# A two-layer block on one core: queries of two heads rounded into one tile, maxima from half-zero keys, halves copied by DMA

## The reference

```
q = (x @ Wq + bq).reshape(B, S, 16, 64)
k = x @ Wk + bk
v = x @ Wv + bv
scores = einsum('bshd,btd->bhst', q, k) / sqrt(64)
w = softmax(scores, axis=-1)
out = einsum('bhst,btd->bshd', w, v).reshape(B, S, 1024) @ Wo + bo
```

## Time and profile before

| | |
|---|---|
| median of 3 runs | 1415.53 us (1414.4 to 1416.4) |
| the profiled execution | 1409.84 us |
| its span, from first to last instruction | 1408.0 us |
| TensorE busy | 1286.0 us, 91% |
| VectorE busy | 1011.7 us, 72% |
| ScalarE busy | 708.6 us, 50% |
| GpSimd busy | 270.9 us, 19% |
| mean clock granted to TensorE | 0.962 of full |
| moved by DMA | 100.25 MB |

### The profile page before, as it was taken

How to read it: one execution, slowest core, us unless ns; L and a number is a source line. 1 busy time by engine, 2 the same in 40 slices (tenths; PEclk the granted TensorE clock), 3 DMA queues, 4 the chain that set the end, 5 groups by cost and what they waited for, 6 DMA issues and landing times.

```text
span 1408.0 us, 22235 instructions
## 1 busy us (share of the span) xinstructions
PE 1286.0 (91%) x7377; PEld 760.0 (54%) x7377; DVE 1011.7 (72%) x2393; ACT 708.6 (50%) x1300; POOL 270.9 (19%) x314
## 2 busy tenths in 40 slices
PE   4569988999989998999899999999999979999997
PEld 2335435554545555555454555555655538686844
DVE  7776866578857875787668766876687747677875
ACT  3126544544464445444554445544545448677741
POOL 3033222200120012001200120012000205454630
PEclk9569998999999999999999999999999989999999
DMA  2051433000210021003000200020000246465451
GB/s 75 0 158 61 151 108 138 29 17 19 84 32 17 18 85 32 18 18 85 31 17 19 85 32 17 18 85 32 18 17 19 62 136 207 155 214 170 144 179 48
DMA packets 69299, 100.25 MB, mean 71 GB/s; under 512 B 29196, under 2 KB 45132, under 8 KB 65220
## 3 DMA queue, kind: packets, MB, share of 16 engines
q1 hardware_dynamic: 54628, 66.23, 15.2%
q0 software_dynamic: 11344, 31.64, 6.9%
q10 hardware_dynamic: 3216, 0.97, 0.3%
HBM read 59.86 MB, written 38.68 MB: 70 GB/s over the span
## 4 chain that ended last, share of the span: by engine, by line
PE 73%; DVE 16%; issue 3%; DMA 2%; ACT 2%; SPq 2%; POOL 1%; DVEq 0%; ACTq 0%; POOLq 0%
PE bank L1420 14%; PE bank L1392 8%; PE bank L1348 7%; PE bank L1431 6%; PE bank L1393 6%; PE bank L1256 5%; PE bank L1258 5%; PE bank L1257 5%; PE bank L1452 4%; DVE mneg L987 3%; PE bank L1272 2%; PE bank L1262 2%; DVE q_lm L981 2%; PE bank L1307 2%; PE bank L1289 1%
## 5 line engine op out<-in xcount | busy, mean ns | idle before, releaser
L815 ACT ACTIVATE wide<-bank 128x512 f32<-128x512 f32 x512 | 301.5, 604 | 493.3 <-PE bank L1393 483.0
L987 DVE TENSOR_REDUCE mneg<-bank 128x1 f32<-128x512 f32 x512 | 347.2, 685 | 182.2 <-PE bank L1348 176.5
L1420 PE MATMUL bank<-wide,v_w 128*32 128x512 f32 x2048 | 249.5, 605 | 0.5 <-issue 0.5
L1348 PE MATMUL bank<-k_hl,q_hh 128*128 128x512 f32 x512 | 208.0, 407 | 34.9 <-DVE mneg L987 21.7
L1392 PE MATMUL bank<-q_hh,k_hl 128*128 128x512 f32 x512 | 234.7, 458 | 1.7 <-ACT wide L815 1.4
L1393 PE MATMUL bank<-q_lm,k_h 65*128 65x512 f32 x512 | 203.6, 398 | 0.0
L1392 PEld LDWEIGHTS bank<-q_hh,k_hl 128*128 128x128 f32 x512 | 97.0, 189 | 131.1 <-issue 89.5
L614 POOL TENSOR_TENSOR rs<-rs,power 128x4 f32<-128x4 f32 x24 | 24.6, 1026 | 626.4 <-DVE rs L889 626.4
L1348 PEld LDWEIGHTS bank<-k_hl,q_hh 128*128 128x128 f32 x512 | 98.1, 192 | 72.6 <-issue 51.7
L1431 PE MATMUL bank<-wide,ones 128*32 128x512 f32 x992 | 129.1, 592 | 0.0
L684 POOL DMA_INDIRECT y_rows<-y_m,to_u x92 | 104.2, 1132 | 127.0 <-DVE y_m L1114 105.1
(11 more groups left out here) (231 smaller groups left out, 1970.4 us busy)
## 6 DMA issues: line engine op xcount, KB each, us to landing
w_t<-w_rows SPq DMA_DIRECT2D x23, 1024.0 KB
x_rows<-part_h POOLq DMA_DIRECT2D x65, 258.0 KB, 6.1
inv<-inverse_scratch SPq DMA_DIRECT2D x124, 128.0 KB, 2.9
w_rows<-w_t SPq DMA_DIRECT2D x8, 1024.0 KB, 4.9
x_m<-x_rows SPq DMA_DIRECT2D x23, 258.0 KB, 3.6
stage<-in_L_ffn_W SPq DMA_DIRECT2D x16, 256.0 KB, 5.2
yab<-y_rows POOLq DMA_DIRECT2D x8, 512.0 KB, 9.4
xin<-in_L_attn_x SPq DMA_DIRECT2D x8, 256.0 KB, 5.9
```

What stands on the lines that cost most here:

```text
L815: act.activation(wide[:, st.g % WIDE, :], ps, ACT.Exp, scale=SCALE1).then_inc(wide_full, 1)
L987: dve.tensor_reduce(mneg[:, (gh // 2) % 2, col:col + 1], ps[:], X, ALU.max, negate=True)\
L1348: into(("mx", gh, j), lambda ps: pe.matmul(ps[:], q_hh[:, gh % HEADS, P * j:P * j + P], k_hl[:, n % 2, :], start=True, stop=True))
L1420: pe.matmul(ps_out[0][rows, :], v_w[:, n, c, TILE * d:TILE * d + TILE], weights, start=(c == 0), stop=(c == TT - 1))
```

## The change

The two heads of a pair are prepared together.

- One projection for a pair instead of one for each head: the weights of two heads stand side by side (`wq_h[:, h:h + 2]`), and the result has the first head in the upper and the second in the lower 64 partitions. It stands at s = 2 of a pair, for the pair after the next (before: heads 4 and 5 later, at s = 1 and 5).
- ScalarE rounds it once, into a new tile `q_x` (two buffers). VectorE subtracts for each head from its half, two instructions together at s = 3, and now ahead of its work for layer 0 in that step.
- SP copies the halves of `q_x` to `q_hh`, both heads to both halves of the partitions: four DMAs a pair. The first scores of a pair wait for them.
- The maxima are taken from `q_x` with keys that are zero in the other head's half (`k_a`, `k_b`), rounded queries with rounded keys alone, without the keys' rest. The products come two at a time in the even steps. ScalarE writes these keys once for each row, two more copies; GpSimd clears the tiles once.
- `x_h` and `x_l` have one buffer instead of two, and `wq_h` and `wq_l` hold the weights once, with half as many splits at the start.
- GpSimd takes some roots earlier in its list: in row 0 ahead of the splits of steps 27 and 45 (before: 33 and 48), and in each row the next row's first root ahead of the clearing.
- The rows of the first expert tiles are loaded at step 6 of row 7 (before: 10). The second half of an output projection moves from step 17 to step 18 after the row, and one copy of layer 0 on ScalarE from step 2 to step 1.

```diff
-    LEAD = 3
+    QUERY_AT = 2
-    WO_AT = [ATT - 10, ATT + 17]
+    WO_AT = [ATT - 10, ATT + 18]
-    L0_AT = {1: -8, 2: -7, 3: -5, 4: -5, 5: -3, 6: -2, 7: -1, 8: -1, 9: 1, 10: 2, 13: 2, 14: 3, 15: 4, 16: 4,
+    L0_AT = {1: -8, 2: -7, 3: -5, 4: -5, 5: -3, 6: -2, 7: -1, 8: -1, 9: 1, 10: 1, 13: 2, 14: 3, 15: 4, 16: 4,
-    ROWS_AT, WEIGHTS_AT = 10, [1, 5, 10, 13]
+    ROWS_AT, WEIGHTS_AT = 6, [1, 5, 10, 13]
...
     def head_events(st):
-        ahead_ = gh + LEAD + s // TT
-        if 0 <= ahead_ < H * NB:
-            events.append(("mx", ahead_, s % TT))
-        if s == TT + 1 and 0 <= gh + 2 < H * NB:
-            events.append(("mt", (gh + 2) // 2))
-        if s % TT == 1 and 0 <= ahead_ + 1 < H * NB:
-            events.append(("q", ahead_ + 1))
+        here, total = gh // 2, H // 2 * NB
+        if s == TT + 1 and 0 <= here + 1 < total:
+            events.append(("mt", here + 1))
+        if s % 2 == 0:
+            pair, j = (here + 1, s // 2 + 2) if s < TT else (here + 2, s // 2 - 2)
+            if 0 <= pair < total:
+                events.append(("mx", pair, j))
+        if s == QUERY_AT and 0 <= here + 2 < total:
+            events.append(("q", here + 2))
...
+            def copy_queries(pair):
+                sp.wait_ge(qx_done, pair + 1)
+                for b in range(2):
+                    gh, here = 2 * pair + b, slice(DK * b, DK * b + DK)
+                    if gh >= HEADS:
+                        sp.wait_ge(first_full, last_step(gh - HEADS) + 1)
+                    for half in range(2):
+                        sp.dma_start(q_hh[DK * half:DK * half + DK, gh % HEADS, :].bitcast(F32), q_x[here, pair % 2, :].bitcast(F32))\
+                          .then_inc(q_copied[pair % 2], 16)
...
             for st in steps:
+                for event in head_events(st):
+                    if event[0] == "q":
+                        copy_queries(event[1])
                 for r, k in row_steps(st):
                     sums_and_inverses(r, k)
...
+            pool.memset(k_a[:].bitcast(F32), 0.0).then_inc(consts, 1)
+            pool.memset(k_b[:].bitcast(F32), 0.0).then_inc(consts, 1)
...
-                if SPLIT_STEPS[j] in (33, 48):
+                if SPLIT_STEPS[j] in (27, 45):
                     root()
...
                 if n + 1 < NB:
+                    root()
                     zero(n + 1)
-                    root()
                 scatter(n)
...
-            def round_q(gh):
-                ps, _ = filled(act, ("q", gh))
-                if gh >= HEADS:
-                    act.wait_ge(first_full, last_step(gh - HEADS) + 1)
-                act.activation(q_hh[:, gh % HEADS, :], ps[:], ACT.Identity, bias=bq[:, gh % H:gh % H + 1])\
-                   .then_inc(qh_done, 1)
+            def round_q(pair):
+                ps, _ = filled(act, ("q", pair))
+                if pair >= 2:
+                    read_out(act, ("q", pair - 2))
+                    act.wait_ge(q_copied[pair % 2], pair // 2 * 64)
+                p = pair % (H // 2)
+                act.activation(q_x[:, pair % 2, :], ps[:], ACT.Identity, bias=bq_two[:, p:p + 1]).then_inc(qx_done, 1)
...
                     act.activation(k_hl[:, n % 2, :], ps[:], ACT.Identity, bias=bk[:, 0:1])
+                    act.activation(k_a[0:DK, n % 2, :], ps[0:DK, :], ACT.Identity, bias=bk[0:DK, 0:1])
+                    act.activation(k_b[DK:, n % 2, :], ps[DK:, :], ACT.Identity, bias=bk[DK:, 0:1])
...
-            def lo_q(gh):
+            def lo_q(pair):
+                ps, free = full(("q", pair))
+                dve.wait_ge(qx_done, pair + 1)
+                for b in range(2):
+                    gh, rows = 2 * pair + b, slice(DK * b, DK * b + DK)
+                    h = gh % H
+                    if gh >= HEADS:
+                        dve.wait_ge(first_full, last_step(gh - HEADS) + 1)
+                    ins = dve.scalar_tensor_tensor(q_lm[0:DK, gh % HEADS, :], ps[rows, :], bq[rows, h:h + 1],
+                                                   q_x[rows, pair % 2, :].bitcast(F32), ALU.add, ALU.subtract)
+                ins.then_inc(free, 1)
...
-                pe.wait_ge(qh_done, gh + 1)
-                into(("mx", gh, j), lambda ps: pe.matmul(ps[:], q_hh[:, gh % HEADS, P * j:P * j + P], k_hl[:, n % 2, :],
-                                                         start=True, stop=True))
+                pe.wait_ge(qx_done, pair + 1)
+                for b, keys in enumerate((k_a, k_b)):
+                    into(("mx", 2 * pair + b, j), lambda ps: pe.matmul(ps[:], q_x[:, pair % 2, P * j:P * j + P], keys[:, n % 2, :],
+                                                                       start=True, stop=True))
...
                     if c == 0:
-                        read_out(pe, ("q", gh))
+                        if gh % 2 == 0:
+                            read_out(pe, ("q", gh // 2))
+                            pe.wait_ge(q_copied[(gh // 2) % 2], (gh // 4 + 1) * 64)
```

More of the change, by code:

```diff
@@ L211, in head_events, with split_pair, head_uses @@
         gh, events = H * st.r + 2 * p, []
[L212 to L226 removed]
+        here, total = gh // 2, H // 2 * NB
[7 more added lines that the diff above has]
+            events.append(("q", here + 2))
+        return events
+    def split_pair(st):
+        if st.kind not in ("pre", "o") or st.k % PAIR != QUERY_AT + 1:
+            return None
+        pair = (H * st.r + 2 * (st.k // PAIR)) // 2 + 2
+        return pair if 0 <= pair < H // 2 * NB else None
+    def head_uses(st):
+        return [use for e in head_events(st)
+                for use in ([("mx", 2 * e[1] + b, e[2]) for b in range(2)] if e[0] == "mx" else [e])]
     def wo_at(r, part):
@@ L802, in _ @@
                         src = raw[:, n, :].rearrange("p (h d) -> p h d", d=DK)
-                        for hi in copies(wq_h[:, 8 * n:8 * n + 8]):
-                            last = act.activation(hi, src, ACT.Identity)
-                        last.then_inc(split_h, 1)
+                        act.activation(wq_h[:, 8 * n:8 * n + 8], src, ACT.Identity).then_inc(split_h, 1)
             act.wait_ge(split_l, 2)
+            act.wait_ge(bias_set, 2)
+            act.wait_ge(consts, N_CONSTS)
             for st in steps:
@@ L1207, in _ @@
             for st in steps:
+                if split_pair(st) is not None:
+                    lo_q(split_pair(st))
                 if st.kind in ("pre", "o"):
@@ L1211, in _ @@
                             next(cuts[n], None)
-                if split_head(st) is not None:
-                    lo_q(split_head(st))
                 for event in head_events(st):
@@ L1358, in fill @@
                         t = slice(P * i, P * i + P)
-                        last = three(ps[:, cols * i:cols * i + cols], x_h[:, n % 2, t], x_l[:, n % 2, t], w_h[:], w_l[:])
+                        last = three(ps[:, cols * i:cols * i + cols], x_h[:, t], x_l[:, t], w_h[:], w_l[:])
                     return last
@@ L1368, in begin @@
                     read_out(pe, ("xt", n))
-                    into(("k", n), lambda ps: three(ps[:], twice(wk_h[:]), twice(wk_l[:]), x_h[:, n % 2, :], x_l[:, n % 2, :]))
+                    into(("k", n), lambda ps: three(ps[:], twice(wk_h[:]), twice(wk_l[:]), x_h[:], x_l[:]))
                 if use == "vg":
```

60 lines of the change are left out of this document (30 added, 30 removed).

## The result

| | before | after |
|---|---|---|
| median | 1415.25 us | 1376.71 us (1370.76 to 1383.24) |
| ratio | | 0.9729, interval 0.9706 to 0.9751 |
| profiled execution | 1409.84 us | 1377.28 us |
| its span | 1408.0 us | 1375.2 us |

The forecast was 1372.5 us, range 1350 to 1397. The time is 4 us above the one and well inside the other. The profile shows that this is partly luck: two of the steps behind it failed (the reuse of a bank in part 3, the copies in part 7), and other terms made up for them.

A forecast was written before the change was run, and what follows sets the result against it. TensorE, busy 91% of the span, was taken to bound the kernel. The terms -45 + 8 + 5 + 8 - 1 - 9 - 9 gave -43 us, so 1372.5 us against a median of 1415.5, range 1350 to 1397.

The forecast's parts named there:

- part 3: VectorE: same work, bank reuse still two steps away; TensorE's saving not collected where VectorE is full: +8 us, bounds 0 and 20.
- part 7: Four copy DMAs a pair on SP's queue: they land well before the scores need them, cost 0.
- Part 1: Query projections on TensorE: half go, 64 triples of matmuls removed, -45 us.
- Part 2: Rounding moves into ScalarE's tight steps: scores of step 5 wait for the exponential, +8 us; extra key copies, +5.
- part 6: First expert rows in the last row, loaded earlier: shorter TensorE idling and no clock drop, -9 us, bounds -13 and -3.
- Part 4: The start: fewer GpSimd subtractions for query weights spare slowed VectorE operations, -1 us, bounds -2 and +2.
- Part 5: Roots in row 0: served at once, -12 us; later split and staging give back 3; -9, bounds -13 and 0.
- Rival C: Scores of step 0 of every pair: late copies on SP's in-order queue make the kernel slower; 1437 us at 1 us beyond; chance 0.05.
- likeliest case: The forecast itself, whole kernel: 1372.5 us, with its own range of 1358 to 1387 us; chance 0.62.
- A: Rival, whole kernel: ScalarE and VectorE take most of the gain, leaving 1388 to 1411 us; chance 0.18.
- B: Rival, whole kernel: roots and rows give all, engines behind take nothing, 1343 to 1358 us; chance 0.12.
- D: Rival, whole kernel: no change, the projection being hidden by something the page does not show; chance 0.03.

The follow-up runs named there:

- y2: The changed kernel with each pair's projection computed twice into the same bank: 1421.3 us, ratio 1.0020 to the kernel before.
- y4: The changed kernel with layer 0's turned hidden tile and its product one step later (33 and 34 for 32 and 33): 1354.0 us, ratio 0.9554.
- y1: The changed kernel with the two half-zero key copies made from the rounded keys, behind the signal VectorE waits for: 1380.8 us, ratio 0.9740.
- x1: The kernel before with only the new order of roots and the first expert rows loaded at step 6: 1391.1 us, ratio 0.9837.
- x2: The changed kernel with the old order of roots and the first expert rows loaded at step 10: 1403.2 us, ratio 0.9896.
- z3: y4 with the first of the two early roots back behind the splits of steps 27 and 30 (33 for 27): 1351.8 us, ratio 0.9584.
- z4: The changed kernel with eight copies a pair instead of four on SP's queue, scores waiting for all: 1395.0 us, ratio 0.9889.
- x4: The changed kernel with the projection at step 1 of a pair instead of step 2: 1373.4 us, ratio 0.9695.
- z2: y4 with the projection at step 1 of a pair: 1369.9 us, ratio 0.9692.

## Why the prediction was right, and where it was not

**Part 1, -45: right.** y2 measures the triple at 0.71 us against my 0.70, and the six rows of y4, with the bank out of the way, are 35.3 us shorter than before, where 48 triples are 34.

**Part 2, the queue, +8: right as a wait.** The scores wait for the exponential 36 times, 9.5 us in all (5 times and 1.4 us before), 0.24 each in a steady row, in 4 pairs of 8. The keys' copies, +5, cost nothing that can be told (y1).

**Part 3, +8: the step that failed.** I wrote that "the closest reuse of a bank is still two steps away, as before". At step 32 it is in the same step. The "as before" was wrong too: in the kernel before the tile refilled a product of the step just before, step 31, and in step 4 layer 0 refilled a product of its own step. I had not followed the ring through the steps of layer 0. That costs 3.5 us a row and 21.2 in the six rows (845.8 less 824.6), against 8 that I had for all of VectorE in the whole kernel. My sign for it, waits for reductions under 3 us a row, failed as well: they are 4.4 in the row shown above (2.1 of them the tile's). Apart from the bank VectorE and ScalarE gave nothing back on balance: in y4 a row gains 6.2 us for 8 triples of 0.71. The waits for the exponential are still there (0.7 us in that row), but TensorE's waits for reductions and subtractions before L1348 (3.7 us in a row before) shrank to 0.8 before L1384. With it failed a sentence of part 6, that "A short wait leaves the clock alone": 2.10 us did so in one row of six.

I had set three terms, 21 us in all, on ScalarE and VectorE; of them 8 were there as waits, and one bank took about the sum. The total came out; its parts did not, and that is luck.

**My own sign.** I had said that I am wrong if a steady row shrinks by less than 3 us or if the chain shows SP or a DMA. The six rows shrank by 2.35 us each (859.9 less 845.8, by six), so by my own sign the account of the rows was wrong. The second sign was badly set, since the kernel before has SP and DMA in its chain too. The chain after, in order of time, runs through SP's copies in row 7 (0.54 to 0.60 us each):

```profile
1109.77 0.54 SPq L537
1110.35 0.60 SPq L537
1110.99 0.60 SPq L537
1111.64 0.60 SPq L537
...
1120.43 3.60 DMA x_m<-x_rows
1124.08 1.11 PE bank L1296 x4
1125.19 0.43 PE bank L1290
```

**Part 4, -1: right in sign.** The two operations of VectorE that I had counted take 0.34 and 0.35 us in after, where GpSimd's subtractions run ahead of them. The first scores start at 111.4 us in the kernel before, at 110.0 in x1, and at 108.3 in after (109.2 in y4): 1 to 3 us, too little to tell from one execution each.

**Part 5, -9: right in kind, larger alone.** x1 gains 12.2 us in row 0, and with the pairs in place (x2 to after) it is 9.8. Two of the three moved roots do it. Of the late staging I had put 3 us on the moved split; z3 finds none there. The weights are late in x2, where no root was moved, and not in x1; z4 makes them later with more copies. So the copies delay them.

**Part 6, -9.** Alone 8.3, between my bounds. The first rows are turned at 1106.09, 17.4 us after the table is set (1088.68), where I had 18; TensorE idles 0.68 us, not 3. But the third tile's rows are issued only at 1120.43, behind the copies and weights, and the idle time is there: 3.50 us at 1124.08, and the clock falls. 0.43 us from one matmul to the next in the rows above, against 0.23 to 0.24 in the steady ones, is the lower of its two levels (1.2 of 2.4 GHz). The Trainium skill has this in "TensorE: Matmul & The Clock Gate", "HAM oscillation": stalls between groups of matmuls drop the clock, so that the work behind each pays again. The trace agrees here (granted clock 0.50 from 1124 to 1128), and in five of the six steady rows, but not in the sixth.

**Part 7, 0: wrong in two rows of eight.** No scores wait for a copy, as I had it, and in the six rows eight copies cost 1.1 us more than four. But SP's queue has other work in row 0 (staging) and in row 7 (the experts' loads), and I had priced only the landing of the copies, not the 2.46 us of issuing four of them (1109.77 to 1112.23 above) ahead of someone else's load. The table gives the size for row 7: x1 to after is +2.4 us, although some of the 64 triples go there too; the second four cost 8.7 more. Rival C had the right queue and the wrong waiter: not the scores, but the tokens' rows and the staged weights.

**The rivals.** The time lies in the likeliest case's own range. A (1388 to 1411) named the right engine, VectorE, for what was lost, but neither the exponential (x4) nor the keys' copies (y1) carries it. B needed the bank to be free: y4 reaches 1354, inside B's range, with one number changed in each of two places. D is excluded by y2.

**What stays open.** Part of row 0: the pairs should gain some 6 us up to its first output and give 0.6 (x1 to after). The tile's bank is 1.4 of the rest, and z4 makes 4 or 5 of it by the copies likely, but the copies were doubled, not taken away. Taking a single product away from step 32 in place of moving the tile was not tried. Nor were three small parts of the change run alone: the output projection at step 18, the copy of layer 0 at step 1, and the single buffer of `x_h` and `x_l` (TensorE waits for `x_l` 3.1 us in all, 1.5 before).

## What to carry to other kernels

When work that goes through a ring of buffers is put together in one step, count the uses of each step against the ring's size: in a step with one use more than buffers the last one needs a bank that was filled in the same step. It costs where the reader is behind (step 32) and nothing where the reader is free (step 24). Where the reader is behind, a reuse one step later can cost as much (z2), and it can lie far from the lines that were changed. A place tuned for one arrangement can be worth as much against the next one (22 us each way here), so move it and measure. And price a DMA on an in-order queue twice: by when it lands, and by what stands behind its issue in the busiest stretch of that queue, not in a typical one.

## What the runs showed of the hardware

- The same wait of 2.10 us, with 0.57 us of waiting before it and the same work around, was followed by the lower clock in five of six rows (granted clock 0.50 to 0.60 over the 4 us behind the wait) and by the full clock in one (0.50 and 1.00 in the rows shown under y4). The waits of one row can't tell whether the clock will fall; the cost differs by up to 3 us from row to row of one execution.
- VectorE's operations of 128x4 numbers, with two inputs each, took 1.24 and 1.19 us instead of 0.16 while GpSimd ran two expert splits (167.91, 2.48 us). VectorE in order of time, row 0 of after:

```profile
167.95 1.24 DVE L922 SCALAR_TENSOR_TENSOR rs<-rs 128x4 f32<-128x4 f32 x1
169.22 1.19 DVE L923 TENSOR_TENSOR rs<-rs 128x4 f32<-128x4 f32 x1
170.44 0.16 DVE L924 SCALAR_TENSOR_TENSOR rs<-rs 128x4 f32<-128x4 f32 x1
```

  Each of the two splits took 1.24 us. The small operation lasts as long as the split beside it, so its size says nothing of its price. The Trainium skill ("GPSIMD Engine Reference", "1. Specifications") says that GpSimd shares its way to the memory with VectorE, and that instructions with two inputs contend; the trace agrees, and puts a factor of 7 on the smallest ones.
